# Last attention of a four-layer conditioned sequence model: Q and K as two fp32r halves, maxima of two heads at a time, three energy banks, lead interleaved with the projections

## The reference, cut to what matters

```python
h = _sln(hidden, w, ...)                       # layer norm, scaled and shifted by the condition
qkv = (h @ Wqkv.T + bqkv).reshape(B, N, 16, 16, 3)
energy = jnp.einsum('bhqd,bhkd->bhqk', q, k)   # B=2, 16 heads, 1024 x 1024 each, d=16
att = jax.nn.softmax(energy, axis=-1) / D ** 0.5
out = jnp.einsum('bhqk,bhkd->bhqd', att, v)
out = out.reshape(B, N, D) @ Wp.T + bp
h1 = out + hidden
return _sln(h1, w, ...) + h1
```

## Time and profile before

| | |
|---|---|
| median of 3 runs | 1095.48 us (1092.41 to 1095.51) |
| span of the profiled execution | 1094.8 us |
| PE busy | 975.0 us, 89% of the span |
| DVE busy | 672.3 us, 61% |
| ACT busy | 450.2 us, 41% |
| POOL busy | 203.2 us, 19% |
| matmuls of maxima and energies | 512 + 512 |
| reductions of 1024 | 256, 301.2 us of DVE |
| exponentials of 512 | 512, 277.7 us of ACT |

### The profile page before, as it was taken

How to read it: one execution, slowest core, us unless ns; L and a number is a source line. 1 busy time by engine, 2 the same in 40 slices (tenths; PEclk the granted TensorE clock), 3 DMA queues, 4 the chain that set the end, 5 groups by cost and what they waited for, 6 DMA issues and landing times.

```text
span 1094.8 us, 12565 instructions
## 1 busy us (share of the span) xinstructions
PE 975.0 (89%) x4724; PEld 512.8 (47%) x4724; DVE 672.3 (61%) x1133; ACT 450.2 (41%) x784; POOL 203.2 (19%) x225
## 2 busy tenths in 40 slices
PE   4698799999997997999997687999999999999973
PEld 0446688955455445978762241333333333333412
DVE  6776867553105216742734746888888888888546
ACT  1110332233331234232120112777777777777660
POOL 2864202020002001200255284000000000000022
PEclk9698899999999998999897595999999999999997
DMA  9242200110000000000029221440504134000011
GB/s 337 88 142 91 79 1 1 40 39 0 1 1 0 1 1 0 1 1 1 1 86 123 23 72 44 59 55 6 59 1 59 28 33 56 4 1 1 2 38 38
DMA packets 29887, 44.15 MB, mean 40 GB/s; under 512 B 6478, under 2 KB 22400, under 8 KB 29570
## 3 DMA queue, kind: packets, MB, share of 16 engines
q1 hardware_dynamic: 28932, 40.22, 17.3%
q0 software_dynamic: 896, 3.15, 0.8%
HBM read 34.70 MB, written 8.39 MB: 39 GB/s over the span
## 4 chain that ended last, share of the span: by engine, by line
PE 75%; DVE 11%; ACT 5%; POOL 4%; issue 2%; DMA 2%; SPq 0%; DVEq 0%; ACTq 0%; POOLq 0%
PE PA L1132 12%; PE PA L1121 11%; PE PD L1091 9%; PE PD L987 8%; PE PA L965 7%; PE PD L910 5%; PE PA L1040 5%; PE PD L1013 5%; PE PA L901 4%; DVE NMX L1568 2%; ACT R L798 2%; PE PD L1056 2%; PE PA L893 2%; DVE ST L1309 2%; PE PD L819 1%
## 5 line engine op out<-in xcount | busy, mean ns | idle before, releaser
L1568 DVE TENSOR_REDUCE NMX<-PD 128x1 f32<-128x1024 f32 x256 | 301.2, 1219 | 64.2 <-PE PD L1091 64.1
L798 ACT ACTIVATE R<-PA 128x512 f32<-128x512 f32 x512 | 277.7, 594 | 93.6 <-PE PA L1121 90.7
L1121 PE MATMUL PA<-R 99*128 99x512 bf16 x512 | 164.2, 389 | 12.1 <-ACT R L798 6.6
L1091 PE MATMUL PD<-R 96*128 96x512 bf16 x512 | 143.5, 400 | 18.6 <-DVE NMX L1568 16.2
L1121 PEld LDWEIGHTS PA<-R 99*128 99x128 bf16 x512 | 42.5, 97 | 171.7 <-ACT R L798 154.0
L987 PE MATMUL PD<-WHR,HSR 128*128 128x256 f32 x512 | 98.5, 292 | 7.4 <-DVE HSR L1487 4.9
L729 ACT ACTIVATE R<-PA,VEC 128x512 f32<-128x512 f32 x64 | 43.7, 688 | 147.7 <-PE PA L965 125.5
L568 POOL TENSOR_SCALAR VE<-MV 128x4 f32<-128x4 f32 x16 | 4.0, 251 | 516.1 <-DVE MV L1312 516.0
L965 PE MATMUL PA<-XSR,WHR 128*128 128x512 f32 x256 | 85.9, 418 | 10.5 <-issue 5.3
L987 PEld LDWEIGHTS PD<-WHR,HSR 128*128 128x128 f32 x512 | 85.7, 199 | 12.2 <-DVE HSR L1487 5.5
L1091 PEld LDWEIGHTS PD<-R 96*128 96x128 bf16 x512 | 48.5, 99 | 89.6 <-DVE NMX L1568 31.3
(11 more groups left out here) (238 smaller groups left out, 1242.0 us busy)
## 6 DMA issues: line engine op xcount, KB each, us to landing
R<-in_l_w SPq DMA_DIRECT2D x8, 1024.0 KB, 5.2
R<-qk_parts SPq DMA_DIRECT2D x48, 128.0 KB, 5.4
R<-qk_parts SPq DMA_DIRECT2D x96, 64.0 KB, 5.6
W<-in_w SPq DMA_DIRECT2D x4, 1024.0 KB, 10.1
R<-in_wcond SPq DMA_DIRECT2D x1, 3584.0 KB, 11.6
qk_parts<-WA SPq DMA_DIRECT2D x8, 384.0 KB, 2.6
qk_parts<-WA POOLq DMA_DIRECT2D x8, 384.0 KB, 3.0
X<-in_x SPq DMA_DIRECT2D x4, 512.0 KB, 14.0
```

The costliest lines, as they stand in the source:

```text
L798: act.activation(PB[:, n % 2, j, :], PA[:, e % 2, :], ACT.Exp).then_inc(s_exp3, 1)
L1091: i = pe.matmul(PDF[:, n % 2, kc * HALF:(kc + 1) * HALF], QS[0:KSTK, gg % NSLOT, c, j, t * P:(t + 1) * P], KS[0:KSTK, gg % NSLOT, j, kc * ...
L1121: pe.matmul(PA[:, e % 2, :], KS[:, gg % NSLOT, j, kt * P:(kt + 1) * P], QS[:, gg % NSLOT, c, j, :], start=True, stop=True).then_inc(s_eful ...
L1568: ve.tensor_reduce(NMX[:, m % 2, r:r + 1], PDF[:, n % 2, :], axis=AX_X, op=ALU.max, negate=True).then_inc(s_mred, 1)
```

## The change

- Q and K are cut into two parts of type fp32r (`high`, written by ACT in that type, and `low`, one DVE operation that reads PSUM and subtracts `high`), and three products are stacked: 3 x 16 = 48 rows, with two rows for the maximum 50. Heads 2j and 2j + 1 lie in the row halves 0 to 63 and 64 to 127 of the stack (`HROW` = 64). POOL has no part in the cutting any more. There are four buffers of parts instead of two.
- A maximum pass is now two heads x 128 queries x 512 keys: one matmul in each row half, each into a bank of its own. DVE's reduction makes two maxima for each partition of 2 x 512, and the two key halves are joined with a minimum at the end of a unit (L1604). The number of matmuls, of reductions and of elements is what it was.
- Three energy banks (`NEB`) instead of two. `times_v` of the step before now stands between energy 2 and energy 3, and the maximum passes on either side of energies 0 and 1 of the next step.
- The transposes of the maxima (`tm`) and of the heads (`ho`) now take a place in the same rotation of two PSUM places as the maximum passes (`pair_bank`): PE waits, before each, for the job two before it. DVE instead of ACT cuts the transposed maxima into their two parts. Four DMAs instead of three write them.
- `LEAD` is 20 instead of 30, and the transpose stands behind step 8m - 2 instead of 8m - 6. The first 20 passes are interleaved with the single projection jobs of batch 1 (`mx`, `qk3`, `v3`). V's projection of this layer goes through the `PA` banks. Ten steps instead of 15 are left without maximum passes.

```diff
-PAIRS = [(0, 0), (0, 1), (1, 0), (1, 1), (0, 2), (2, 0)]
-KSTK = NPAIR * HD
-NPART = 3
+TERMS = [(0, 0), (0, 1), (1, 0)]
+NROW = 2
+HROW = P // NROW
+KSTK = len(TERMS) * HD
+NPART = 2
-LEAD = UNIT + 14
+LEAD = UNIT + 4
+NEB = 3
+def turn_step(m):
+    return (UNIT * m + (UNIT + 1 if m < NUNIT - 1 else UNIT - 1) - LEAD) // 2
+SOLO = turn_step(NUNIT - 1) + 1
...
             for m in range(NUNIT):
                 gg, c = divmod(m, NC)
-                sp.wait_ge(s_nmt, m + 1)
-                for s in range(NPART):
-                    sp.dma_start(QS[KSTK + s:KSTK + s + 1, gg % NSLOT, c],
-                                 NMT[s * UNIT:(s + 1) * UNIT, :]).then_inc(s_nmrow[m % 4], 16)
+                sp.wait_ge(s_mred, MJ[("turn", m)] + 1)
+                for jj in range(JJ):
+                    for s in range(NPART):
+                        sp.dma_start(QS[KSTK + s:P:HROW, gg % NSLOT, jj, c * HALF:(c + 1) * HALF].bitcast(F32),
+                                     NMT[jj * NROW * TPC:(jj + 1) * NROW * TPC, s, :].bitcast(F32)
+                                     ).then_inc(s_nmrow[m % 4], 16)
...
+            def pair_bank(*job):
+                n = MJ[job]
+                if n >= 2:
+                    pe.wait_ge(s_mred, n - 1)
+                return n % 2 * 2
+            def maxpass(n):
+                o = pair_bank("max", n)
+                q0 = c * HALF + t * P
+                for h in range(NROW):
+                    rows = slice(h * HROW, h * HROW + KSTK)
+                    i = pe.matmul(PD[:, o + h, :], QS[rows, gg % NSLOT, jj, q0:q0 + P],
+                                  KS[rows, gg % NSLOT, jj, kc * HALF:(kc + 1) * HALF], start=True, stop=True)
+                i.then_inc(s_mfull, 1)
             def turn_max(m):
+                pe.wait_ge(s_nmc, m + 1)
+                o = pair_bank("turn", m)
+                pe.transpose(PD[0:UNIT, o, 0:P], NMC[:, :], ident[:, :]).then_inc(s_mfull, 1)
...
                 energy(n, 2)
+                if n >= 1:
+                    times_v(n - 1)
                 energy(n, 3)
-                if n > SOLO:
-                    times_v(n - 1)
-                if s < NMAX:
-                    maxpass(s)
-                    maxpass(s + 1)
+                more = max_jobs("step", n)
+                for _, x in more[:1]:
+                    maxpass(x)
                 if n + 1 < NSTEP:
                     if kt == NT - 1:
                         nmrow_in(pe, m + 1)
                     energy(n + 1, 0)
                     energy(n + 1, 1)
+                for _, x in more[1:]:
+                    maxpass(x)
...
+            def turned_max(m):
+                o = PD[0:UNIT, pair_bank("turn", m), 0:P]
+                link(ve.tensor_copy(NMT[:, 0, :], o))
+                ve.tensor_tensor(NMT[:, 1, :], o, NMT[:, 0, :], ALU.subtract).then_inc(s_mred, 1)
```

More of the change, by code:

```diff
@@ L136, in act_jobs @@
     if stage == "qk3":
-        return [(b, w, c, k) for k in range(KB) for w in ("q3", "k3") for c in range(NC)]
+        b, j = divmod(b, QJOBS)
+        k, r = divmod(j, 2 * NC)
+        side, c = divmod(r, NC)
+        return [(b, "qk3", side, c, k)]
+    if stage == "v3":
+        b, j = divmod(b, TWO)
+        return [(b, "v3", j)]
     return []
@@ L162, in dve_jobs, with max_jobs @@
         return [(0, "ot", b, k) for k in range(KB)]
-    out = {"y0": "y0", "qkv": "v1", "pr": "pr", "f2": "f2", "qk3": "v3"}.get(stage)
+    if stage == "hd":
+        return [(b, "hd")]
+    out = {"y0": "y0", "qkv": "v1", "pr": "pr", "f2": "f2"}.get(stage)
     return [(b, out, j) for j in range(TWO)] if out else []
+def max_jobs(stage, n):
+    if stage == "mx":
+        return [("max", n)]
+    if stage == "step":
+        return [("max", LEAD + 2 * n + i) for i in range(2) if LEAD + 2 * n + i < NMAX]
+    return [("turn", n)] if stage == "tm" else [("heads", n)] if stage == "ho" else []
 def number(jobs_of):
@@ L302, in build, with parts @@
         O = [XN[:, b] for b in range(B)]
[L304 to L308, removed]
+        def parts(j):
+            return PARTS[j % NPARTS // 2][:, j % 2]
         PA = ctx.enter_context(nc.psum_tensor("PA", [P, 4, HALF], F32))
@@ L418, in run @@
                     engine_stages[stage](b)
-        QK3_JOBS = [(name, c, k) for k in range(KB) for name in ("q3", "k3") for c in range(NC)]
         block = ctx.enter_context(nc.Block())
@@ new lines, in v3 @@
+            def v3(j):
+                b, j = divmod(j, TWO)
+                n = AJ[(b, "v3", j)]
+                if b == 0 and j == 0:
+                    ve.wait_ge(s_dfull, DJ[(1, "w21", NT - 1)] + 1)
+                ve.wait_ge(s_afull, n + 1)
+                for u in range(2):
+                    i = ve.tensor_tensor(VP[b][:, 2 * j + u, :, 0:HD],
+                                         PA[:, n % 4, u * D:(u + 1) * D].rearrange("p (h d) -> p h d", h=HEADS),
+                                         BC[:, BV3, :].rearrange("p (h d) -> p h d", h=HEADS), ALU.add)
+                i.then_inc(s_aev, 1)
@@ L1615, in turned_first, with heads_paired, heads_single @@
+            def heads_paired(m):
+                norm_heads_out(m, PD[:, pair_bank("heads", m), :], s_mred)
+            def heads_single(m):
+                norm_heads_out(m, bank(m, "hd"), s_dev)
+            def step(n):
+                for _, x in max_jobs("step", n):
+                    reduce_max(x)
             def turned_first(h):
```

398 lines of the change are left out of this document (176 added, 222 removed).

## The result

The changed kernel takes **1185.34 us** (median of 4 runs, 1182.89 to 1186.4) where the kernel before takes 1095.49 (1092.41 to 1096.28) beside it. The ratio is 1.0816 with a 95% interval of 1.0791 to 1.0841: 8.2% slower, and outside the range that was predicted (1062 to 1138). The profiled execution has a span of 1183.6 us, with a granted clock of 0.847 on the mean over the span where before had 0.932.

What follows compares the result with a forecast made beforehand. PE, busy 39.85 of 40 us amid the steps, was taken as the bound. From 1094.8 us, 39.3 less ahead of the steps and 35.0 more in them gave 1090.5, with 0.7 for the median 1091; range 1062 to 1138.

Steps and rivals of the forecast that it cites:

- The regular step, 2.45: A step without extras takes 2.45 us, set by a loop from `times_v` through energy 3, exponential and energy 2.
- The row halves run together, 0.12 a matmul: In a step, matmuls in the two row halves run side by side, each costing 0.12 us.
- Copy to `UO` +0.6: Once a unit, the copy waits for a later `times_v` and delays the exponentials, adding 0.6 us.
- The maxima's transpose +1.15: Once a unit, the transpose of the maxima waits for the step's first reduction, adding 1.15 us.
- The heads' transposes +1.25: Once a unit, the transposes of heads wait for the step's first reduction, adding 1.25 us.
- The wait for the rows, +2.95: Once a unit, PE waits before energy 0 for the DMAs of the maxima's rows, adding 2.95 us (2.9 to 3.3).
- The clock, +1.5 for a unit: After each wait for the rows, energy 0 to the end of `times_v` runs at 1.2 GHz, adding 1.5 us (0 to 1.7).
- the 31.4 for start and end: Start-up of the steps, 3 us, and the nine further steps to the last energy, 28.4 us.
- a mean clock below 0.85 over the steps: Sign that the prediction is wrong, listed beside matmuls 0.2 apart and no idle stretch before a unit's first energy.
- The lead, -39.3: Ahead of the steps, the first energy comes near 634.5 us where it was 673.8, a gain of 39.3 us.
- the clock falls for longer stretches: Rival: PE idles in every unit, so half the steps run at 1.2 GHz, 77 us more: 1168 us, chance 0.08.
- the rival with 0.13, rows in time: Rival: the maxima's rows land before PE needs them, no idle stretch or slow clock, 62 us less: 1028 us, chance 0.13.

Runs made afterwards that it cites:

- the run with the second pass twice: The changed kernel, lead still 20, with the pair of fp32r matmuls of each step's second maximum pass issued twice: 1151.81 us in one run.
- The run with PE busy 95% at 0.50 for 416 us: The changed kernel, lead still 20, with one overwritten bf16 matmul of 512 columns on all 128 rows added to each step: 1347.27 us in one run.
- the two kernels of the last windows: The changed kernel with one bf16 matmul on all rows added to a step (1347.27 us), and with both maximum passes issued twice (1124.3 us).

## Why the prediction was wrong, step by step

- **The regular step, 2.45: 2.61.** The loop that was named is the one that bounds, and two of its terms were short. Energy 3 to its exponential is 0.53 (910.46 to 910.99 in the trace), not 0.45, and energy 2 to `times_v` 0.43 (911.64 to 912.07), not 0.32. A matmul that starts a new layout of the array takes 0.49 to its end where one behind its like takes 0.39. The way back from the exponential was 0.06 (911.58 to 911.64) and not 0.09. 118 x 0.16 = 19 us.
- **The row halves run together, 0.12 a matmul: right,** as far as the pairs show it (0.23 from one pair to the next).
- **Copy to `UO` +0.6: +0.58** (step of 3.19). **The maxima's transpose +1.15: +1.15** (3.76). **The heads' transposes +1.25: +1.45** (4.06).
- **The wait for the rows, +2.95: +2.6,** in each of the 14 units, ended by the DMA from `NMT`, as foretold. A step with the wait takes 5.22 in the one unit of the run with the second pass twice in which the clock stayed up.
- **The clock, +1.5 for a unit: this is the step that failed.** The measured terms at full clock are 118 x 2.61 = 308, 14 x (0.58 + 1.15 + 1.45 + 2.6) = 81, and the 31.4 for start and end as predicted (not measured by themselves), together 420. 510.5 were measured, so the clock costs 90, **6.4 in a unit**. The 118 steps alone took 473.7 where these terms give 389, so 85 of the 90 are in them. The windows give the same by another way: over 507 us of steps the clock is 0.74 on the mean, so it is 0.50 for 52% of them, 264 us, and a regular step does in 4.07 there what it does in 2.61 elsewhere, so 264 x (1 - 2.61/4.07) = 95. The lead of 24 is the test of it. I had taken the length of the slow stretch, 3.4 us, from the earlier trace rows: stretches behind idle time in quite other code. The row was right for that code and said nothing of how this step would recover: behind the waits the clock stayed at 0.50 for 10 to 24 us, which is several steps and not one `times_v`. The prediction had named a mean clock below 0.85 over the steps as a sign of being wrong; it is 0.74.
- **The lead, -39.3: -37.6.** First energy 636.2 for 634.5. `f2` ended at 588.3 for 588.5. What the first energy came behind was in part another thing than foretold: the four DMAs of the rows were issued from 631.4 on, and with the 3.24 us that pass from there to the energy in a unit (916.72 to 919.96) the rows would have been there near 634.6, an estimate; PE was still in V's projection until 635.1 and then in two passes.
- **The rivals.** The one with 0.08, "the clock falls for longer stretches", was the case. The clock was at 1.2 GHz for half of the time. That its 1168 came within 17 us is in part luck: the regular step added 19 and the heads' transposes 3, but its clock, 21 + 77 = 98, was 8 too dear, and the wait 5; 6 more came behind the last energy and 2 in the lead. Its chance was too small. I had before me that PE would idle 14 times in 425 us and that the clock falls each time, and gave no thought to what a recovery asks for; a range that took it in would have held the time. That the rows come late was its condition, and the rival with 0.13, rows in time, is what two more passes of lead make true. It gives 1073 and not 1028. Of these 45 us the regular step explains 19, the heads' transposes 3, the first energy at 639.9 and not 634.5 another 5, and 4 come behind the last energy; the rest, some 14, was not taken apart, and the two falls of the clock are in it.

The Trainium skill (TensorE: Matmul & The Clock Gate, What's actually happening) says that the clock follows how busy PE has been of late. The run with PE busy 95% at 0.50 for 416 us shows that the busy time in a profile is not the measure; the rule gives no way to tell the two kernels of the last windows apart. It also says (TensorEngine Tiling (Array Packing), Key Properties) that a change of tiling mode drains the engine. The traces agree: at half clock 0.56 pass before the matmul on all rows starts and 0.54 until the next, where one pair of matmuls in row halves follows another after 0.43 (881.55 to 881.97).

## What to carry to other kernels

A short regular wait of PE must be priced with the clock behind it, and that price isn't in the wait: behind waits of 2.1 to 2.4 us it ran from nothing to 24 us at half clock, by the steps around them. Where a lead is cut, count what lies between the producer and the first wait on it, and try two passes more: here a wait of 2.6 us in a unit cost 8.4 us of steps (510.5 against 392.9 with a lead of 24, over 14 units), and a lead of 22 in place of 20 gave back 112. And a helper's small transposes belong behind work that is ready, not ahead of it: here the later place was worth 24 us, 17 of them in the steps with transposes.

## What the runs showed of the hardware that was not expected

- After a wait of 2.4 us the clock stayed at 0.50 for 10 to 24 us with PE busy 23.32 of 23.9, and with one matmul on all rows in a step for 416 us.
- A wait of 2.37 us brought no fall at all in the second unit of the two kernels with one pair added, and with a lead of 22 the clock once fell to 0.50 behind idle time of no more than 0.93 us in one piece.
- Matmuls that are not needed made the kernel faster: two pairs more in each step, 61 us (1185.3 to 1124.3), with the regular step longer by 0.04 on the mean.
- A single matmul on all rows between matmuls in row halves costs 0.26 to 0.35 at full clock and 1.06 to 1.24 at half clock. A pair of the same columns in row halves cost nothing at full clock.
- Two matmuls in different row halves start within 3 ns of each other and end together, as at 910.46.
